# Gated attention block on one core: means subtracted by GpSimd, weights rounded by VectorE, one load moved up

## What is computed

```
x1 = x  + tanh(g_xattn) * attention(layernorm(x), ctx, ctx, mask, W1, b1, W2, b2)
y  = x1 + tanh(g_ffn)   * mlp(layernorm(x1), w1, b1, w2, b2)

attention(q, k, v, mask):   qp, kp = proj(q), proj(k)        # proj: x W1^T + b1, then W2^T, + b2
                            softmax(qp kp^T / sqrt(128) + mask) v
mlp(z):                     h = relu(quant(quant(z) wq1 + bq1));  quant(h) wq2 + bq2
quant(z) = clip(round(16 z), -128, 127) / 16     # of weights and biases with 64 in place of 16
layernorm(z) = (z - mean) / sqrt(var + 1e-5)
```

## Time and profile before

| what | value |
|---|---|
| median of 3 runs | 66.66 us (66.5 to 66.83) |
| the profiled execution's own time | 66.68 us |
| its span | 64.9 us |
| busy in the span | PE 57.8, PEld 45.9, VectorE 54.7, ScalarE 52.4, GpSimd 44.5 us |
| read from HBM, written | 6.88 MB, 2.10 MB |

### The profile page before, as it was taken

How to read it: one execution, slowest core, us unless ns; L and a number is a source line. 1 busy time by engine, 2 the same in 40 slices (tenths; PEclk the granted TensorE clock), 3 DMA queues, 4 the chain that set the end, 5 groups by cost and what they waited for, 6 DMA issues and landing times.

```text
span 64.9 us, 1898 instructions
## 1 busy us (share of the span) xinstructions
PE 57.8 (89%) x565; PEld 45.9 (71%) x565; DVE 54.7 (84%) x308; ACT 52.4 (81%) x145; POOL 44.5 (69%) x92
## 2 busy tenths in 40 slices
PE   4999799768999899999999999999999899996830
PEld 4988574517877788795979899699696779464510
DVE  4569959496999899999799999999999998888620
ACT  2600889849999979999999999999999969769600
POOL 5958888994790894698999999906997949133000
PEclk9999999999999999999999999999999999999999
DMA  0899999999980000000000003120300403041232
GB/s 0 231 412 405 416 414 406 414 400 408 406 324 23 0 0 5 10 0 0 10 0 0 0 5 119 58 111 0 128 34 0 169 8 144 18 162 73 93 121 81
DMA packets 3324, 9.09 MB, mean 140 GB/s; under 512 B 369, under 2 KB 754, under 8 KB 3314
## 3 DMA queue, kind: packets, MB, share of 16 engines
q1 hardware_dynamic: 3312, 8.98, 35.9%
q10 hardware_dynamic: 2, 0.00, 0.0%
HBM read 6.88 MB, written 2.10 MB: 138 GB/s over the span
## 4 chain that ended last, share of the span: by engine, by line
POOL 38%; issue 14%; DMA 14%; ACT 10%; DVE 9%; PE 4%; SPq 4%; POOLq 1%; ACTq 1%; DVEq 0%
POOL xq L377 17%; DMA load_sb<-in_packed 14%; POOL rs L359 12%; ACT pr L597 4%; POOL xn L367 4%; SPq L326 4%; DVE st L641 3%; POOL rs L355 2%; ACT prT L606 2%; PE bank_A L483 2%; DVE load_sb L707 2%; PE bank_O L524 2%; ACT xn L573 1%; DVE mv L644 1%; ACTq L149 1%
## 5 line engine op out<-in xcount | busy, mean ns | idle before, releaser
L624 ACT ACTIVATE h<-bank_H,fb_q 128x512 int8<-128x512 f32 (+2 forms) x28 | 16.2, 645 | 2.2 <-PE bank_H L509 2.1
L641 DVE BATCH_NORM_STATS2 st<-load_sb 128x6 f32<-128x128 f32 x64 | 14.0, 279 | 2.4 <-DMA load_sb<-in_packed 2.3
L359 POOL TENSOR_TENSOR rs<-ve,half 128x4 f32<-128x4 f32 (+2 forms) x9 | 8.5, 941 | 9.3 <-DVE nm L648 9.3
L597 ACT ACTIVATE pr<-sc,mn 128x120 f32<-128x120 f32 x32 | 12.4, 408 | 0.9 <-DVE mn L695 0.9
L377 POOL TENSOR_SCALAR xq<-load_sb,nm,rs 128x128 int8<-128x128 f32 x28 | 12.3, 456 | 0.8 <-POOL rs L359 0.2
L355 POOL TENSOR_TENSOR rs<-ve,half 128x4 f32<-128x4 f32 (+2 forms) x9 | 8.5, 942 | 2.6 <-DVE nm L648 2.6
L367 POOL TENSOR_SCALAR xn<-load_sb,nm,rs 128x128 f32<-128x128 f32 x22 | 9.6, 448 | 0.5
L467 PEld LDWEIGHTS bank_S<-kpT,xaT 128*128 128x128 f32 x64 | 8.1, 191 | 2.6 <-issue 2.3
L483 PE MATMUL bank_A<-load_sb,prT 120*128 120x128 f32 x64 | 9.1, 283 | 0.3 <-ACT prT L606 0.3
L707 DVE SCALAR_TENSOR_TENSOR load_sb<-bank_A,rec,load_sb 128x128 f32<-128x128 f32 x32 | 9.1, 343 | 0.4 <-DVE rec L700 0.3
L524 PE MATMUL bank_O<-w_q,h 128*128 128x128 bf16 x128 | 9.2, 219 | 0.2
(11 more groups left out here) (80 smaller groups left out, 102.0 us busy)
## 6 DMA issues: line engine op xcount, KB each, us to landing
load_sb<-in_packed SPq DMA_DIRECT2D x6, 496.0 KB, 8.0
out_y<-y_sb SPq DMA_DIRECT2D x6, 256.0 KB, 2.0
load_sb<-in_packed SPq DMA_DIRECT2D x2, 512.0 KB, 11.0
load_sb<-in_packed SPq DMA_DIRECT2D x1, 576.0 KB, 14.2
load_sb<-in_packed SPq DMA_DIRECT2D x1, 514.0 KB, 6.1
load_sb<-in_packed SPq DMA_DIRECT2D x1, 448.0 KB, 5.3
load_sb<-in_packed SPq DMA_DIRECT2D x1, 432.0 KB, 12.7
load_sb<-in_packed SPq DMA_DIRECT2D x1, 428.0 KB, 13.3
```

The source lines that it names most:

```text
L359: nc.gpsimd.tensor_tensor(rs2[:, of(g, n=1)], ve2[:, of(g, n=1)], half[:, of(g, n=1)], ALU.pow).then_inc(rs2_done, 1)
L597: nc.scalar.activation(pr[i][:, j, :], sc[i][:, j, :], ACT.Exp, scale=-1.0, bias=mn[:, of(g, j, 1)], accum_out=den[:, of(g, j, 1)]).then_i ...
L624: nc.scalar.activation(low_byte(h16[g % RING], hcols(c, g)), bank_H[c][:, cols(g)], ACT.Relu, bias=fb1_q[:, c:c + 1]).then_inc(h_act[c], 1)
L641: nc.vector.bn_stats(st[:, START[g] + j, :], x_of(g, j)).then_inc(st_done, 1)
```

## The change

- GpSimd subtracts the mean in its normalising and quantising instructions (it added the negated mean before), so that `nm` is no longer computed; `rstd1` and `rstd2` wait for `ve` alone, and `scale_means` negates for itself.
- `scale_weights` moves from ScalarE to VectorE, with the same three instructions as multiplications.
- The load of ("k", 2) and ("x", 3) moves from place 6 to place 4, ahead of the first two groups of v and of the MLP's weights.
- The groups become 2, 4, 4, 4, 4, 4, 4, 3, 3 tiles; the shares, the order of the stages and the fillers are new.

With it the loads are 257, 436, 496, 496, 384, 514, 496, 512, 496, 496, 512, 432, 552 and 640 KB. The tiles that ScalarE normalises go from 7 to 3, those of VectorE from 3 to 6, those of GpSimd from 22 to 23; VectorE quantises 6 tiles where it did 4, and takes one more relu chunk (of group 8). VectorE's order from the first x is: stats1(0), fold_cp1, stats1(1), fold_cp2, stats1(2), normalise_dve(1), stats1(3), row_maxima(0), scale_means(2), scale_weights, scale_means(3), reciprocals(0), normalise_dve(2), stats1(4), row_maxima(1), residual(0), stats1(5).

```diff
-TILES = [3, 4, 4, 4, 4, 4, 4, 3, 2]
+TILES = [2, 4, 4, 4, 4, 4, 4, 3, 3]
...
+    [("k", 2), ("x", 3)],
     [("v", 0), ("v", 1)],
     [("mlp",)],
-    [("k", 2), ("x", 3)],
...
-XN_ON_POOL = [1, 2, 3, 2, 4, 3, 2, 3, 2]
-XN_ON_ACT = [2, 2, 1, 2, 0, 0, 0, 0, 0]
-XQ_ON_POOL = [1, 3, 4, 4, 4, 4, 4, 3, 1]
-RELU_ON_ACT = [4, 4, 3, 3, 2, 3, 3, 3, 3]
+XN_ON_POOL = [2, 3, 2, 2, 4, 3, 2, 3, 2]
+XN_ON_ACT = [0, 0, 1, 2, 0, 0, 0, 0, 0]
+XQ_ON_POOL = [0, 3, 4, 4, 3, 4, 4, 3, 1]
+RELU_ON_ACT = [4, 4, 3, 3, 2, 3, 3, 3, 2]
...
-    stats1=[375, 485, 715, 977, 1110, 1325, 1569, 2218, 3232],
+    stats1=[380, 548, 701, 851, 1245, 1508, 1802, 2450, 3329],
-    fold_cp1=[627],
+    fold_cp1=[460],
-    scale_weights=[845],
+    scale_weights=[1040],
-    row_maxima=[1244, 1470, 1921, 2513, 2868, 3151, 3630, 4255, 4573],
+    row_maxima=[979, 1370, 1632, 2103, 2560, 3139, 3555, 4088, 4353],
...
-FILLERS = [8, 38, 19, 5]
+FILLERS = [9, 26, 7, 8, 14]
...
-                pool.wait_ge(ve1_done, 2 * end)
+                pool.wait_ge(ve1_done, end)
...
-                    nc.gpsimd.tensor_scalar(xn[g % RING][:, tile(j)], x_of(g, j), nm1[:, of(g, j, 1)],
-                                            rs1[:, of(g, j, 1)], ALU.add, ALU.mult).then_inc(xn_pool, 1)
+                    nc.gpsimd.tensor_scalar(xn[g % RING][:, tile(j)], x_of(g, j), mv1[:, START[g] + j, 0:1],
+                                            rs1[:, of(g, j, 1)], ALU.subtract, ALU.mult).then_inc(xn_pool, 1)
...
-                nc.vector.tensor_scalar(nm[:, at], mv[:, at, 0], -1.0, None, ALU.mult).then_inc(ve_done, 1)
...
-                nc.vector.tensor_tensor(nr1[:, of(g, n=1)], nm1[:, of(g, n=1)], rs1[:, of(g, n=1)],
-                                        ALU.mult).then_inc(nr1_done, 1)
+                nc.vector.scalar_tensor_tensor(out=nr1[:, of(g, n=1)], in0=mv1[:, of(g, n=1), 0], scalar=-1.0,
+                                               in1=rs1[:, of(g, n=1)], op0=ALU.mult, op1=ALU.mult).then_inc(nr1_done, 1)
...
+            def scale_weights():
+
+                wait_load(dve, "mlp")
+                nc.vector.tensor_scalar(mp_8[:, :], mp_sb[:, :], W_SCALE, None, ALU.mult).then_inc(quant8, 1)
+                dve.wait_ge(row_in, 16)
+                nc.vector.tensor_scalar(fb2_8[:, :], row_sb[:, 2:2 + D], W_SCALE, None, ALU.mult).then_inc(quant8, 1)
+                dve.wait_ge(quant8, 1)
+                nc.vector.tensor_scalar(w1_q[:, :], mp_8[:, 0:C * P], 1.0 / W_SCALE, None, ALU.mult).then_inc(w1_up, 1)
```

More of the change, by code:

```diff
@@ new lines @@
+    stats1=[380, 548, 701, 851, 1245, 1508, 1802, 2450, 3329],
+    fold_mm1=[386],
+    fold_cp1=[460],
+    rstd1=[473, 686, 926, 1037, 1383, 1887, 1998, 2584, 3441],
+    normalise_pool=[553, 797, 1148, 1504, 1600, 2119, 2930, 3027, 3840],
+    fold_mm2=[567],
+    spread_gates=[606],
+    transpose_x=[624, 934, 1260, 1639, 1999, 2362, 3060, 3434, 3985],
+    fold_cp2=[672],
+    copy_xT=[685, 999, 1348, 1712, 2064, 2455, 3164, 3588, 4108],
+    negate_mask=[711],
+    project_keys=[713, 755, 1069, 1419, 1820, 2141, 2540, 3234, 3697],
@@ new lines @@
+    copy_keys=[774, 857, 1177, 1562, 1922, 2245, 2926, 3367, 3888],
+    normalise_dve=[0, 826, 1206, 0, 0, 2311, 2952, 0, 3833],
+    scores=[839, 1155, 1504, 1906, 2410, 2838, 3299, 3851, 4223],
+    gate=[912],
+    row_maxima=[979, 1370, 1632, 2103, 2560, 3139, 3555, 4088, 4353],
+    scale_means=[0, 0, 1032, 1191],
+    scale_weights=[1040],
+    copy_ident=[1047],
+    normalise_act=[0, 0, 1063, 1233],
+    exponentials=[1101, 1409, 1760, 2302, 2725, 3214, 3677, 4198, 4604],
+    reciprocals=[1198, 1793, 2037, 2549, 3003, 3705, 4216, 4343, 5060],
@@ new lines @@
+    widen_weights=[1235],
+    transpose_probs=[1236, 1587, 2078, 2493, 2925, 3382, 3914, 4431, 4776],
+    copy_probsT=[1313, 1652, 2143, 2558, 2990, 3528, 4049, 4505, 4905],
+    attend=[1371, 1732, 2224, 2638, 3106, 3608, 4132, 4579, 5037],
+    residual=[1456, 1934, 2347, 2802, 3225, 3727, 4239, 4679, 5144],
+    stats2=[1714, 2184, 2642, 3012, 3427, 3961, 4482, 4892, 5235],
+    rstd2=[1806, 2473, 2809, 3329, 3719, 4099, 4620, 5004, 5347],
+    fold_base=[2048],
+    quantise_dve=[2049, 2769, 0, 0, 3935, 0, 0, 0, 5471],
@@ new lines @@
+    transpose_xq=[2127, 2785, 3583, 3960, 4406, 4811, 5104, 5361, 5639],
+    copy_base=[2200],
+    copy_xqT=[2216, 2876, 3627, 4148, 4554, 4855, 5167, 5460, 5717],
+    split_base=[2248],
+    hidden=[2315, 2969, 3757, 4283, 4643, 4946, 5238, 5532, 5776],
+    relu0=[2511, 3412, 3828, 4327, 4720, 4989, 5281, 5570, 5814],
+    relu2=[2615, 3104, 3989, 4446, 0, 5108, 5400, 5668],
+    relu3=[2651, 3469],
+    quantise_pool=[0, 2680, 3156, 3546, 3937, 4220, 4741, 5110, 5453],
+    relu1=[2687, 3047, 3932, 4386, 4780, 5048, 5341, 5619, 5863],
@@ L109 @@
+    mlp_out=[2726, 3467, 4017, 4464, 4834, 5126, 5420, 5656, 5863],
+    result=[2910, 3641, 4151, 4610, 4996, 5336, 5554, 5792, 6008],
+    relu_dve3=[0, 0, 3867, 4417, 4827, 5071, 5403, 5620, 5900],
+    relu_dve2=[0, 0, 0, 0, 4759, 0, 0, 0, 5848],
+    keep_warm0=[385.5],
+    keep_warm1=[566.5],
+    keep_warm2=[712.5],
+    keep_warm3=[933.5],
+    keep_warm4=[1068.5],
 )
-FILLERS = [8, 38, 19, 5]
+FILLERS = [9, 26, 7, 8, 14]
 class Share(list):
```

31 lines of the change are left out of this document (11 added, 20 removed).

## The result

The changed kernel takes 73.59 us (median of 4 runs, 72.82 to 74.28) where the kernel before took 66.75 beside it (66.5 to 67.11): a ratio of 1.0915, 95% interval 1.0825 to 1.1004. By the ratio it is slower by 6.1 us (by the two medians 6.8), where 1.7 us less had been forecast. The profiled execution took 72.95 us, its span is 71.1 us.

What follows compares the result with a forecast made beforehand. VectorE's nearly full queue was taken as the bound, with idle at the head not regained. Its terms gave -2.18 us at residual(8), the tail +0.4 and +0.1: -1.7 us in all, 66.68 to 65.0 us, range 64.0 to 66.4.

Steps and rivals of the forecast that it cites:

- The cover: GpSimd's 9.3 us of waiting for `nm`, taken as slack should its subtraction, priced at nothing, cost more.
- first x: First load at the head, 64 KB smaller: -0.1 us (ends 0 and -0.2).
- the weights: Three weight instructions moved onto VectorE's queue: +1.5 us, with ends of 1.3 and 2.3.
- groups (stats2, residual, result): One tile moves from group 0 to group 8, so VectorE has less before residual(8): -0.7 us.
- Idle of the head: VectorE's load waits, its wait in `scale_means` and some other idle go: -2.4 us (ends -1.3 and -3.7).
- No `nm`: VectorE drops the negated means, 17 slots before residual(8) and half of one long hold: -1.36 us.
- The tail: From residual(8) to the end, 8.40 us before: +0.4 us for group 8's three tiles, +0.1 for its larger store.
- The total: Whole kernel: -1.7 us, 65.0 us in place of 66.68.
- A: Rival: all VectorE idle goes and the weights are cheap, 63.7 or 64.2 us; chance 0.14.
- B: Rival: the late landing falls on the weights' load, VectorE waits, and weights cost 2.0 us: 65.9 us; chance 0.18.
- C: Rival: ScalarE's order paces 30 to 50 us, only 1.0 of 2.4 us idle stays won: 66.4 us; chance 0.10.
- D: Rival: VectorE and GpSimd block each other, eight instructions waiting 0.3 us each: +2.4 us, 67.4 us; chance 0.08.

Runs made afterwards that it cites:

- e2: Kernel before, with `nm` a copy of the mean that GpSimd subtracts instead of adding the negated mean: 75.29 us, ratio 1.1257 to the kernel before.
- e5: Kernel before, with eight forms of one GpSimd instruction run four times each behind its end: 447 ns add and multiply, 602 single operations, 788 to 793 other pairs.
- e1: Changed kernel with the addition back on GpSimd and the 18 `nm` back on VectorE: 65.53 us, ratio 0.9802 to the kernel before.
- e7: e1 with the load of ("k", 2) and ("x", 3) back behind the values and weights: 67.56 us, ratio 1.0109 to the kernel before.
- e12: e1 with one more fill of 1,024 columns on VectorE just ahead of residual(3): 67.07 us, ratio 1.002 to the kernel before.
- e4: Changed kernel, but GpSimd negates the means in a small instruction of its own and adds them: 65.17 us, ratio 0.977 to the kernel before.
- e9: Changed kernel, but one VectorE instruction makes `ve` and the negated mean, which GpSimd adds: 65.36 us, ratio 0.9813 to the kernel before.

## Why the prediction was wrong, and where it was right

**The step that failed** is "Subtracting on GpSimd I cost at nothing: same form, same sizes. Its cover is the 9.3 us of waiting; without it even 20 ns a tile over 49 tiles would be 1.0 us". It was the same instruction on the same sizes, but with another pair of operations, and that alone raised it from 0.45 to 0.79 us, by some 0.34 us a tile (e2, e5). I had taken the price of one form for that of another and gave it no bounds, although the rows held no GpSimd subtraction at all. The cover was named rightly and exceeded: up to the end of its last quantised tile GpSimd idles 55.65 - 44.6 = 11.1 us in e1, and 64.19 - 61.7 = 2.5 us in the changed kernel. So of 17.1 us more work, 8.6 went into idle time and 8.5 moved that end; what follows it is 0.9 us shorter, which makes the 7.6 us between the two spans. The lower clock and TensorE's waits come on the way there and don't hold GpSimd up: of the 2.5 us that it still idles, 1.3 lie before its first reciprocal root at 4.53 us, and behind that no wait of it is listed, only gaps, 1.2 us in 59.7.

The page of the kernel before had a row that warned of it, the shares of the chain that ended last:

```profile
POOL 38%; issue 14%; DMA 14%; ACT 10%; DVE 9%; PE 4%; SPq 4%; POOLq 1%; ACTq 1%; DVEq 0%
```

GpSimd's quantised and normalised tiles are 17% and 4% of it, 13.6 of 64.9 us. At 0.79 in place of 0.45 us that is an estimate of 10 us more; e2 took 8.4 us more (75.29 against 66.90). An engine with idle time can still stand on the chain, and the sum of its waits did not say which of them cover a longer tile.

**The rest of the sum**, judged on e1, comes out at -1.3 us. At residual(8) it is where it was forecast by luck, since the misses there cancel. The terms of e1 are read from VectorE's timeline: the distances from start to start, added up for each operation up to residual(8), less the gaps.

| term, us | forecast | e1 against before |
|---|---|---|
| idle time | -2.4 | -2.39 (3.69 to 1.30) |
| first x | -0.1 | -0.02 |
| `scale_means` | -0.16 | -0.19 |
| `xn`, three tiles more | +0.78 | +0.96 |
| `xq`, one tile more | +0.26 | +0.23 |
| the weights | +1.5 | +1.08 |
| groups (stats2, residual, result) | -0.7 | -0.80 |
| `ve` and `nm`, as many as before | none | -0.80 |
| other small ones | none | -0.29 |
| sum to residual(8) | -0.82 | -2.22 |

(The forecast's sum stands here without its -1.36 for `nm`, which e1 keeps.) Residual(8) starts at 52.09 us in e1, where 52.1 was forecast; but that forecast had counted on saving the `nm`. For e1 its terms give 54.31 - 0.82 = 53.5 us.

- *Idle of the head* was right in size and cause. The waits went as said, but for 0.20 us that stats1(5) still waits for its load in e1, and e7 and e12 show that a wait at the head arrives at the end nearly in full.
- *No `nm`* was right for the slots (1.36 us forecast, 1.34 went in e4), and no gain of it is shown: the time of e4 can't be told from e1's. In e4's profile 0.75 us came back as longer `ve` and quantised tiles, and 0.53 us are the late x of group 2, which e1's execution was spared. What the same small instructions cost is not fixed either: 3.73 us for 34 of them in the kernel before, 2.93 in e1. Why they were held less there was not tried.
- *The weights* I had priced 0.42 us too dear. I had argued from the two rows of 128 columns that SBUF might be no faster. The first instruction took 691 ns for 1,028 columns, less than the relu's 741 for 512 from PSUM, and the three lasted 0.69 + 0.21 + 0.41 = 1.31 us. The Trainium skill (VectorE: DVE Perf Modes, The perf-mode tier table) led to an estimate of 1.35 us; by that rule, the trace agrees, and the page was nearer than my term.
- *The tail* is 61.21 - 52.09 = 9.1 us in e1, against 8.40 + 0.4 forecast; `hidden` of groups 6 and 7 is 2.93 us apart (53.06 and 55.99), where it was 2.78 in the kernel before and was said to stay. `hidden` of group 6 starts 0.97 us after residual(8), where it was 0.78. These two, 0.15 and 0.19 us, are about what the tail is too long by.
- *The total* without the subtraction is 0.980 of the kernel before in e1, -1.3 us, against -1.7. e4 and e9, which have no `nm` on VectorE and so are nearest to what the forecast priced, come to -1.5 and -1.2 us.

**The rivals.** A (all idle goes) did not come: 1.3 us of it stayed. B (the late landing moves to the weights) did not either: no wait for that load shows in e1. C (given back in the middle) is refuted by e7 and e12. D named the right side and the wrong mechanism. The meetings it speaks of are there (0.95 us for 0.33 in e9), but single. That the two engines block each other, as the Trainium skill (Advanced Engine Details and Errata, VectorE Performance Modes) has it, fits the pair of rows of e9. D had to be worth 2 us to decide; what VectorE's instructions last beyond the median of their form, counted from 100 ns up, is 0.3 us in the changed kernel, 0.6 in e1 and 1.0 in e9. What was missing was a rival on GpSimd's own account: all its tiles dearer by some share. At 11 us of idle and 49 tiles it begins to count at some 0.2 us a tile, and earlier where the idle time lies in the wrong places.

## What to carry to other kernels

An algebraic rewrite that only swaps an operation (add a negated value, or subtract it) is a new instruction for GpSimd: take its price from a row of the very same pair of operations, or measure four of them behind the end of the kernel before it goes into every tile. Here one rewrite of 49 instructions turned a 2% gain into a 9% loss, and the good part of the change was only visible once it was taken apart. Where an engine has slack, compare it with the count times a doubling of the price, not with the change in price that one hopes for.

## What the runs showed of the hardware

- GpSimd's two-scalar instruction on 128x128 f32 takes 447 ns with an addition and a multiplication in either order, 602 ns with a single operation, and 788 to 793 ns with the three other pairs tried (e5, medians of four). One operation alone is dearer than the right two.
- Single instructions grow where VectorE and GpSimd work at once: an `xn` tile on VectorE 952 ns in place of 334 in e9, and in the changed kernel a quantised tile on GpSimd 1,029 ns in place of 796, beside two `xn` tiles of VectorE.
- With one order of loads, the x of group 2 was there at 6.81 us in e9 without a wait, and let stats1(2) start only at 7.51 us in e4, 7.61 in the changed kernel and 7.96 in e12. As such a wait passed on to the end in e12, an estimate is that it moves an execution by up to 1 us, more than most of the terms above.
- In the changed kernel TensorE's granted clock fell to its lower level after waits of 0.5 to 0.8 us for single tiles between 30 and 33 us: it was 0.68 from 33 to 34 us, 0.50 from 34 to 36, 0.62 from 36 to 37, and 1.00 again behind that.
